# A fused two-FFN and attention block on one core: a blank first write, weight splits at other places, six low parts on VectorE, and another order while the first stream is alone

## The reference

```python
x = x + 0.5 * ffn(layernorm(x))
x = x + attention(layernorm(x))
x = x + 0.5 * ffn(layernorm(x))

def ffn(x):                       # router: 8 experts, widths 4 x 128 and 4 x 256
    probs = sigmoid(x @ router_w.T)
    topw, sel = top_k(probs, 2); topw = topw / (topw.sum(-1) + 1e-20)
    combine = sum over the two of topw * onehot(sel)
    h = square(relu(einsum('td,edw->tew', x, W1e)))
    return einsum('ted,te->td', einsum('tew,ewd->ted', h, W2e), combine)

def attention(x):                 # 16 heads of 8
    q, k, v = split(x @ W_qkv); q, k = rope(q), rope(k)
    q_feat, k_feat = elu(q * SCALE) + 1, elu(k) + 1
    kv, k_sum = einsum('bhtd,bhtv->bhdv', k_feat, v), k_feat.sum(over t)
    out = einsum('bhtd,bhdv->bhtv', q_feat, kv) / max(q_feat . k_sum, 1e-6)
    return out @ W_out
```

## Time and profile before

| | us |
|---|---|
| median of three runs | 774.62 |
| lowest and highest run | 771.1, 775.65 |
| the profiled execution, its own time | 772.65 |
| its span, from the first to the last instruction | 770.8 |
| PE busy | 724.6 |
| POOL (GpSimd) busy | 685.4 |
| ACT (ScalarE) busy | 602.0 |
| DVE (VectorE) busy | 584.3 |

### The profile page before, as it was taken

The page is one execution under the profiler, slowest core; times in us unless marked ns, Lnnn a source line. Parts: engine busy times, 40 slices in busy tenths (PEclk is TensorE's granted clock), DMA queues, the critical chain, the costliest instruction groups (busy, mean ns, idle before and its releaser), DMA issues.

```text
span 770.8 us, 13299 instructions
## 1 busy us (share of the span) xinstructions
PE 724.6 (94%) x3736; PEld 592.4 (77%) x3736; DVE 584.3 (76%) x1834; ACT 602.0 (78%) x1221; POOL 685.4 (89%) x663
## 2 busy tenths in 40 slices
PE   6899888789999999999999999999999999899888
PEld 6677676668888878888888888888887877777666
DVE  4767887887778797978778797978778587785554
ACT  4688767587888889788888889788878776767876
POOL 3899887879999999999999999999999877686986
PEclk9999999999999999999999999999999999999999
DMA  5553303212233332213333331323333302123331
GB/s 185 192 194 111 111 3 109 95 44 87 107 111 124 111 125 107 77 63 101 123 111 124 111 125 48 114 76 110 124 111 124 112 14 111 36 90 124 122 110 43
DMA packets 31176, 79.38 MB, mean 103 GB/s; under 512 B 3328, under 2 KB 14464, under 8 KB 31104
## 3 DMA queue, kind: packets, MB, share of 16 engines
q1 hardware_dynamic: 30816, 78.47, 29.9%
q10 hardware_dynamic: 288, 0.07, 0.1%
HBM read 73.81 MB, written 4.72 MB: 102 GB/s over the span
## 4 chain that ended last, share of the span: by engine, by line
PE 29%; DVE 27%; POOL 16%; issue 13%; ACT 11%; DMA 3%; DVEq 1%; POOLq 0%; ACTq 0%; SPq 0%
POOL h_lo L942 9%; DVE hid L1129 7%; PE bank L532 4%; PE bank L534 3%; PE bank L533 3%; PE bank L555 3%; POOL root_f L934 3%; PE bank L557 3%; PE bank L556 3%; ACT h_hi L792 3%; ACT hid L781 3%; DVE pick_f L1107 2%; DMA g_all_f<-rows_f 2%; PE bank L651 2%; PE bank L639 2%
## 5 line engine op out<-in xcount | busy, mean ns | idle before, releaser
L942 POOL TENSOR_TENSOR h_lo<-hid,h_hi 128x512 fp32r<-128x512 f32 x383 | 492.1, 1310 | 47.1 <-ACT h_hi L792 46.3
L1129 DVE SCALAR_TENSOR_TENSOR hid<-bank,g_all_f 128x512 f32<-128x512 f32 x384 | 262.6, 684 | 126.0 <-PE bank L534 87.9
L781 ACT ACTIVATE hid<-hid 128x512 f32<-128x512 f32 x384 | 229.6, 621 | 26.7 <-DVE hid L1129 26.1
L792 ACT ACTIVATE h_hi<-hid 128x512 fp32r<-128x512 f32 x384 | 229.0, 622 | 9.0 <-ACT hid L781 0.8
L532 PE MATMUL bank<-x_hi_f,w_hi 128*128 128x512 f32 x384 | 163.9, 427 | 13.5 <-DVE hid L1129 13.4
L555 PE MATMUL bank<-h_hi,w_hi 128*128 128x512 f32 x384 | 153.5, 400 | 4.7 <-POOL h_lo L942 4.5
L557 PE MATMUL bank<-h_hi,w_lo 128*128 128x512 f32 x384 | 152.1, 396 | 0.0
L534 PE MATMUL bank<-x_hi_f,w_lo 128*128 128x512 f32 x384 | 151.6, 395 | 0.0
L533 PE MATMUL bank<-x_lo_f,w_hi 128*128 128x512 f32 x384 | 151.5, 395 | 0.0
L556 PE MATMUL bank<-h_lo,w_hi 128*128 128x512 f32 x384 | 151.3, 394 | 0.0
L532 PEld LDWEIGHTS bank<-x_hi_f,w_hi 128*128 128x128 f32 x384 | 72.8, 190 | 37.4 <-DVE hid L1129 20.7
(11 more groups left out here) (118 smaller groups left out, 1050.4 us busy)
## 6 DMA issues: line engine op xcount, KB each, us to landing
g_all_f<-rows_f SPq DMA_DIRECT2D x128, 512.0 KB, 5.5
x_sb<-in_x SPq DMA_DIRECT2D x16, 256.0 KB, 3.4
out_x<-x_sb SPq DMA_DIRECT2D x15, 256.0 KB, 7.0
g_all_f<-in_w SPq DMA_DIRECT2D x2, 768.0 KB, 6.8
con<-in_const SPq DMA_DIRECT2D x1, 584.0 KB, 6.3
rows_f<-g_row_f SPq DMA_DIRECT2D x32, 16.0 KB, 1.4
out_x<-x_sb SPq DMA_DIRECT2D x2, 128.0 KB, 1.8
g_all_f<-in_wqkv SPq DMA_DIRECT2D x1, 192.0 KB, 6.5
```

Source lines behind the costliest of these rows:

```text
L781: fn(h, h, ACT.Square).then_inc(s_sq[s], 1)
L792: fn(h_hi[:, c, :], hid[:, c % STAGE, :], ACT.Copy).then_inc(s_hhi[s], 1)
L942: gp.tensor_tensor(h_lo[:, c, :], hid[:, c % STAGE, :], h_hi[:, c, :].bitcast(F32), ALU.subtract).then_inc(s_hlo[s], 1)
L1129: v.scalar_tensor_tensor(hid[:, c % STAGE, :], hp[c % 2][:], 0.0, g_all[s][:, EXPERT[c], :], ALU.max, ALU.mult).then_inc(s_z[s], 1)
```

## The change

- A tile `blank` of 32 x 128 zeros is set by VectorE as its first instruction; SP writes it to the HBM buffer of f1's rows after the first two loads of x and w1's load, and waits for its landing before the first real write of rows.
- w1's high part on ScalarE moves from the end of t = -3 to t = -2, behind the exponentials of group 0. Its low part on VectorE moves from t = -3 to t = -2, behind `spread_roots` of group 0.
- The attention weights are split at the top of t = 0 instead of t = -1.
- For groups 0, 1 and 2 of f1, the low parts of chunks 5 and 11 are made by VectorE (`remainder`): chunk 5 after place 14 of its own iteration, chunk 11 after place 3 of the next. POOL leaves them out. They have a semaphore of their own, `s_dlo`; the waits on `s_hlo` count less by them, and who needs them waits for `s_dlo` as well.
- `keep_busy`: 27 instead of 36 at first, 24 instead of 16 in t = -1.
- Where f1 is alone and attention runs (t = 2 and 3), VectorE's order is another: q_features and the first `weighted` ahead of k_features; mask_state before place 4's chunk; normalise's second step right behind its first; add_attention behind place 16 instead of 18.

```diff
+DVE_LOW_GROUPS, DVE_LOW_CHUNKS = range(3), (5, 11)
...
+        blank = sb("blank", [EXP * TG, P])
...
+        def low_on_dve(s, n, c):
+
+            return s == "f1" and n in DVE_LOW_GROUPS and c in DVE_LOW_CHUNKS
+
+        def lows(s, m):
+
+            return m - sum(low_on_dve(s, k // NC, k % NC) for k in range(m))
+
+        def dve_lows(s, m):
+
+            return m - lows(s, m)
...
+                if first_time(s == "f1", n):
+                    sp.wait_ge(s_blank_out, 16)
...
             load(1, 1)
+            sp.wait_ge(s_blank, 1)
+            sp.dma_start(rows["f1"].rearrange("e (k p) -> (e k) p", k=TG), blank[:]).then_inc(s_blank_out, 16)
             sp.dma_start(con[:, first_part:], const[:, first_part:]).then_inc(s_con, 16)
...
-                    pe.wait_ge(s_hlo[s], value(n * NC + c + 1))
+                    pe.wait_ge(s_hlo[s], lows(s, n * NC + c + 1))
+                if low_on_dve(s, n, c):
+                    pe.wait_ge(s_dlo, dve_lows(s, n * NC + c + 1))
...
-            keep_busy(a2, 36)
+            keep_busy(a2, 27)
...
                 if first_time(True, t + 1):
-                    keep_busy(a2, 16)
+                    keep_busy(a2, 24)
...
                 exp_logits("f1", t + 2)
+                if first_time(True, t + 2):
+                    act.wait_ge(s_w1, 16)
+                    fn(w1_hi[:], w1_raw, ACT.Copy).then_inc(s_w1hi, 1)
...
-                if first_time(True, t + 3):
-                    act.wait_ge(s_w1, 16)
-                    fn(w1_hi[:], w1_raw, ACT.Copy).then_inc(s_w1hi, 1)
...
-                        if final(s, n) and c == NC - 1:
+                        if final(s, n) and c == NC - 1 or low_on_dve(s, n, c):
                             continue
...
+            v.memset(blank[:], 0.0).then_inc(s_blank, 1)
...
-                        dve.wait_ge(s_hlo[s], value(m))
+                        dve.wait_ge(s_hlo[s], lows(s, m))
+                        if s == "f1":
+                            dve.wait_ge(s_dlo, dve_lows(s, m))
...
+            def remainder(n, c):
+
+                if live(n) and low_on_dve("f1", n, c):
+                    dve.wait_ge(s_hhi["f1"], n * NC + c + 1)
+                    v.tensor_tensor(h_lo[:, c, :], hid[:, c % STAGE, :], h_hi[:, c, :].bitcast(F32),
+                                    ALU.subtract).then_inc(s_dlo, 1)
...
-                if first_time(True, t + 1):
+                if first_time(True, t):
                     split_attention_weights()
...
-                k_features(t - 2)
-                q_features(t - 2)
-                weighted(t, 0)
+                if alone("f1", t):
+                    q_features(t - 2)
+                    weighted(t, 0)
+                    k_features(t - 2)
+                else:
+                    k_features(t - 2)
+                    q_features(t - 2)
+                    weighted(t, 0)
...
                 weighted(t, 3)
+                remainder(t, 11)
                 stats("f1", t + 3, (par + 1) % 2)
+                if alone("f1", t):
+                    mask_state(t - 2)
                 weighted(t, 4)
                 take_sigmoid("f1", n1)
                 mean_variance("f1", t + 3)
-                if first_time(True, t + 3):
-                    split_w1()
-                mask_state(t - 2)
+                if not alone("f1", t):
+                    mask_state(t - 2)
...
                 normalise(t - 2, 0)
+                if alone("f1", t):
+                    normalise(t - 2, 1)
                 weigh_two("f1", n1, 0)
                 weighted(t, 8)
-                normalise(t - 2, 1)
+                if not alone("f1", t):
+                    normalise(t - 2, 1)
...
                 spread_roots("f1", n1, 1)
                 if first_time(True, t + 2):
+                    split_w1()
+                if first_time(True, t + 2):
                     stats_ahead()
                 weighted(t, 14)
+                remainder(t + 1, 5)
...
                 weighted(t, 16)
+                if alone("f1", t):
+                    add_attention(t - 2)
                 take_sigmoid("f2", n2)
...
                 weighted(t, 18)
-                add_attention(t - 2)
+                if not alone("f1", t):
+                    add_attention(t - 2)
```

More of the change, by code:

```diff
@@ L282, in build @@
         s_zero, s_pconst, s_set, s_floor = sem("s_zero"), sem("s_pconst"), sem("s_set"), sem("s_floor")
+        s_blank, s_blank_out = sem("s_blank"), sem("s_blank_out")
         def per(name, keys):
@@ L323, in build @@
         s_x = per("x", FFN)
+        s_dlo = sem("s_dlo")
         s_lo_last, s_yT_last, s_x_last = sem("s_lo_last"), sem("s_yT_last"), sem("s_x_last")
@@ L1123, in weighted @@
                     if due(m):
-                        dve.wait_ge(s_hlo[s], value(m))
+                        dve.wait_ge(s_hlo[s], lows(s, m))
+                        if s == "f1":
+                            dve.wait_ge(s_dlo, dve_lows(s, m))
                     m = turns(s, t - ago) * NC + (c - STAGE + 1)
                     if c < STAGE and due(m):
-                        dve.wait_ge(s_hlo[other[s]], value(m))
+                        dve.wait_ge(s_hlo[other[s]], lows(other[s], m))
+                        if s == "f2":
+                            dve.wait_ge(s_dlo, dve_lows("f1", m))
                     dve.wait_ge(s_p1[s], value(n * NC + c + 1))
```

## The result

The change takes 770.89 us (median of 18 runs, 768.66 to 773.1) against 773.58 us for the kernel before in runs beside them (770.94 to 776.98): a ratio of 0.9965, 95% interval 0.9954 to 0.9976. So it won 2.7 us, 1.9 to 3.6, where 5.5 were forecast. Its profiled execution took 772.23 us, with a span of 770.4; the one before took 772.65 with a span of 770.8.

The account below looks back on a forecast made before the run. PE, busy 94% of the span, was taken as the bound. Start 2.5, attention split 0, low parts 0.5 and order 2.5 sum to 5.5 us; 773.6 less that gives 768.1 us, range 763.8 to 772.6.

Parts of the forecast that it names:

- the start: Before 30 us, up to POOL's first h_lo: the edits there win 2.5 us, or 1.15 without the blank's effect.
- the order: VectorE's new order at t = 2 and 3: forecast to win 2.5 us together.
- the low parts: Six low parts moved from POOL to DVE, groups 0 to 2: forecast to win 0.5 us, bounds -1.5 to +2.1.
- it looks like a price of a first write: First write of rows, 3.57 us: a blank write pays the price early, so 2.17 us go from the write.
- The attention split: Split moved from t = -1 to t = 0, into DVE's wait for group 1's broadcast: 0 taken, between -0.6 and 0.
- the two about cancel: At t = 1, hid 1 coming 1.0 us earlier is offset by chunk 11 meeting x_lo and pushing the statistics back.
- The rule that I had weighed there: VectorE and GpSimd block each other on SBUF: each of six low parts costs DVE 1.0 us more.
- The mask: mask_state before chunk 2's hid at t = 2 and 3: removes PE's kvm waits, twice 1.05 us.
- q_features and the first hid ahead of k_features: At t = 2 and 3 they fill DVE's 0.79 us idle gap: state comes earlier, twice 0.2 us.
- add_attention early: Two chunks earlier at t = 2 and 3: PE then waits for a hid instead; 0 taken, at most 1.5 us.
- DVE becomes the bound: Rival, t = 0 to 2: low parts cost 10 us, net 8 us slower, about 781 us; chance 0.04.
- A low clock after 24 us, over work that counts: Sign that the forecast is wrong; the earlier low stretch lay over the idle start; no size given.

## Why the prediction was half right

By medians the three parts are: the start 2.2 us (0.9972), the order 3.9 us (0.9949), the low parts -3.4 us (0.9965 less 0.9921). Their sum is the 2.7 us measured, and the start and the order together (0.0079) are just what the kernel without low parts won (0.9921). The agreement is closer than the intervals of 1 to 1.5 us on each part could promise.

**The start, 2.5 forecast, 2.2 measured.** The steps in time came out within 0.4 us each, down to POOL being next and not the hid. The step that failed is the blank write, "it looks like a price of a first write": the write was slow because an instruction fetch fell among its packets. The size survived by luck, because the earlier write misses the fetch anyway. Of the 3.1 us that the first h_lo came earlier, 1.8 is this meeting missed; against an execution of the old start without a meeting (27.55) the edits give 1.3 us at this point, near the 1.15 forecast for the case without the blank's effect. But by the third write only about 0.3 us of that is left (58.25 on the mean against 58.6), so "start: 2.5" also took a lead at the first h_lo for one that lasts. What takes it back wasn't tested. My reason for turning down other traffic, a DMA share of 0.09 in the earlier trace rows, was in good part the fetch itself: one engine of sixteen, held throughout, is a share of 0.06.

**The attention split, 0 forecast, 0 measured.** But "at the old place it would now hold up the first hid" isn't borne out: 0.2 us later in one execution, within what executions differ by.

**Six low parts, +0.5 forecast, -3.4 measured** (1.5 either way, from the two intervals; 1.9 on the mean in the traces). This is the term that failed, and it is larger than all the others' errors. Its bounds, -1.5 to 2.1, were built from POOL's waits on one side and from durations on the other, and both readings were off. PE's waits for POOL are waits for the chunk at hand; taking chunks 5 and 11 from POOL shortened them by 0.5 us out of 2.1. And a low part on DVE isn't only 0.94 to 1.41 us long, it also stands in DVE's queue. Chunk 11's delays the third hid of the next group, by 1.0 us in group 1; PE meets that in group 2 as a wait for the hid itself, and in group 1 as a longer wait for POOL's h_lo, which stands behind a root that waits for DVE's late routing weights. Chunk 5's lengthens the wait for kf by 0.7 us. What the delayed statistics cost through the next group's normalisation wasn't tested. I had seen it push the statistics back and had charged that against an earlier x_hi cast ("the two about cancel"); I hadn't charged the third hid. The rule that I had weighed there, each low part at its blocked price, would have had the sign right: by it six cost up to 6 us of DVE time, and the rows show an excess of 0.25 to 0.7 us each, 2.9 in all, besides 0.69 for the work itself.

**The order, 2.5 forecast, 3.9 measured** (4.0 in the traces). The mask was 2.1 and measured 2.5. q_features and the first hid ahead of k_features were taken at 0.4, and the other three moves together gave 1.4: PE's wait for qf, 3.0 us in two places, became 0.9 for kf and 0.9 that the profile calls issue, and the one for DVE's attn fell from 1.4 to 0.4, while ACT's attn took 1.1 of it back. I had priced this move by DVE's idle 0.79 us of the earlier trace rows and never looked at PE's wait for qf, which is not among. add_attention early: 0 forecast, 0 measured, and for the reason given, that PE then waits for a hid instead.

**The rival "DVE becomes the bound"** had the right place (VectorE from t = 0 to 2) and the right sign for that part, and three times its size (10 against 3.4 us). Its deciding point was wrong: the loss came without DVE's idle time being used up (DVE is idle for 4.7 of 30 us from 30 to 60 us in the change), from low parts in front of an operation that PE hung on.

**The clock.** "A low clock after 24 us, over work that counts" came twice, and cost the profiled execution 2.1 us at 153 to 158 and 1.7 near 748. No edit's median shows it, and the kernel before paid for one in its second execution. The mean clock of the runs is lower with the change (0.9925 against 0.9941), so more time was spent at the low level; how much of it lay over work that counts would need many more profiled executions.

## What to carry to other kernels

Before work is moved to an engine with idle time, look at what stands behind it in that engine's queue at that very place: the low part of chunk 11, one place too early, cost 1.0 us in one group (1.6 by the medians, in three), and all six together relieved PE's waits for POOL by 0.5. A single slow transfer is checked against the packets of all queues, instruction fetches among them, before a cause is written beside it. Before a low clock is blamed for lost time, check whether the engine had a wait behind that stretch that takes it up. And of the waits in a region, sum all those that end in the order that is changed, not those whose names it touches.

## What was not expected of the hardware

- A fetch of instructions is a DMA packet of 0.02 MB that holds one of 16 DMA engines for 0.93 to 1.38 us (at 19.7 to 20.6 us in all sixteen profiled executions). A write of 48 small packets that met one and is waited for as a whole took 3.2 and 3.6 us instead of 1.5, which is 0.7 to 0.8 us more than the fetch it met (0.96 and 1.38).
- A DVE subtraction of 128x512 with both inputs in SBUF took 0.94 to 0.96 us beside POOL's h_lo series and 1.38 to 1.41 behind the start of its x_lo, in the same kernel; one place later the latter took 0.68, and POOL's h_lo that began beside two of them took 1.84 and 1.71 instead of 1.30.
- The same PE gap of 4.7 us with a low clock near it had a price of 2 us in two executions and none in six. Where the low stretch lay over the first 4.8 us behind the gap alone, PE's next wait for hid shrank from 2.5 us to as little as 0.6 and nothing was lost; where it reached beyond, the work behind was late by about half of the part that did. A low stretch came near waits of 2.2 and 2.5 us in the kernel before as well.
